# Attention of a Perceiver block: the score maxima of a batch in one VectorE operation over two PSUM banks

## The reference, cut to what matters

```
scores = einsum('bhsr,bhlr->bhsl', q_r, k_r)       # 16 heads x 32 tokens = 512 rows, 257 keys
attn   = softmax(scores, axis=-1)
ctx_c  = einsum('bhsl,bld->bhsd', attn, kv_rope)
out    = (ctx_c folded with w_kc_kv) @ Wo.T
x      = x + out
```

## Time and profile before

| | |
|---|---|
| median of 3 runs | 1026.26 us (1024.33 to 1026.9) |
| the profiled execution | 1022.87 us, of it a span of 1021.1 us between its first and last instruction |
| attention, from the first maxima to the last batch's exponentials | 139 to 362 us of the span |
| busy over the whole span | PE 94%, DVE 54%, ACT 41%, POOL 44% |

### The profile page before, as it was taken

The page is one execution under the profiler, slowest core; times in us unless marked ns, Lnnn a source line. Parts: engine busy times, 40 slices in busy tenths (PEclk is TensorE's granted clock), DMA queues, the critical chain, the costliest instruction groups (busy, mean ns, idle before and its releaser), DMA issues. The chain is left out here.

```text
span 1021.1 us, 15950 instructions
## 1 busy us (share of the span) xinstructions
PE 955.3 (94%) x5479; PEld 805.6 (79%) x5479; DVE 556.1 (54%) x1040; ACT 411.1 (40%) x954; POOL 453.3 (44%) x489
## 2 busy tenths in 40 slices
PE   4899976999999988999999999889999999999997
PEld 4677755888787866888888988677778899999997
DVE  6333468888899944444545332317968333333345
ACT  2333467677677734223432044352333122222111
POOL 1998845555576620000000302217614878993051
PEclk9999989999999999999999999999999999999999
DMA  6788702111111004422221014312023756661152
GB/s 221 231 269 264 225 13 93 35 40 42 32 37 38 27 27 130 139 83 82 82 89 36 3 59 138 102 29 81 2 85 113 262 171 235 202 225 63 42 159 99
DMA packets 79003, 109.91 MB, mean 108 GB/s; under 512 B 14224, under 2 KB 46992, under 8 KB 78928
## 3 DMA queue, kind: packets, MB, share of 16 engines
q1 hardware_dynamic: 66288, 82.18, 25.9%
q10 hardware_dynamic: 10080, 18.35, 5.0%
q0 software_dynamic: 2560, 8.39, 2.5%
HBM read 83.13 MB, written 25.77 MB: 107 GB/s over the span
## 5 line engine op out<-in xcount | busy, mean ns | idle before, releaser
L43 PE MATMUL psum<-second_xT_hi,second_w_hi 128*128 128x512 f32 x272 | 107.6, 396 | 7.0 <-DVE second_w_lo L1259 3.8
L45 PE MATMUL psum<-second_xT_hi,second_w_lo 128*128 128x512 f32 x272 | 106.6, 392 | 0.0
L44 PE MATMUL psum<-second_xT_lo,second_w_hi 128*128 128x512 f32 x272 | 106.5, 392 | 0.0
L1152 POOL TENSOR_TENSOR all_x<-all_x,mlp_raw 128x512 f32<-128x512 f32 x8 | 10.0, 1290 | 174.7 <-DVE all_x L1654 174.7
L2172 ACT ACTIVATE moe_s<-psum 128x352 f32<-128x352 f32 x39 | 18.1, 465 | 151.0 <-PE psum L45 151.0
L43 PEld LDWEIGHTS psum<-second_xT_hi,second_w_hi 128*128 128x128 f32 x272 | 51.4, 189 | 20.0 <-DVE second_w_lo L1259 5.3
L2238 DVE TENSOR_TENSOR moe_hT_lo<-psum,moe_hT_hi 128x384 fp32r<-128x384 f32 x39 | 21.8, 558 | 79.1 <-ACT moe_hT_hi L2178 79.1
L1609 ACT ACTIVATE mlp_s<-psum,mlp_side 128x512 f32<-128x512 f32 x32 | 21.8, 682 | 100.3 <-PE psum L45 100.3
L43 PE MATMUL psum<-moe_w_hi,moe_tT_hi 128*128 x184 | 61.3, 333 | 0.0
L1654 DVE TENSOR_TENSOR all_x<-all_x,psum 128x512 f32<-128x512 f32 x64 | 43.8, 687 | 31.7 <-PE psum L45 31.2
L45 PEld LDWEIGHTS psum<-second_xT_hi,second_w_lo 128*128 128x128 f32 x272 | 51.4, 189 | 11.0
(11 more groups left out here) (341 smaller groups left out, 2887.0 us busy)
## 6 DMA issues: line engine op xcount, KB each, us to landing
kv_all<-all_x ACTq DMA_DIRECT2D x28, 256.0 KB, 4.1
far_raw<-in_eg SPq DMA_DIRECT2D x10, 704.0 KB, 4.6
far_raw<-in_eu SPq DMA_DIRECT2D x10, 704.0 KB, 4.6
slot_rows<-mix_W SPq DMA_DIRECT2D x23, 256.0 KB, 5.9
slot_out<-far_rows ACTq DMA_DIRECT2D x23, 256.0 KB, 2.4
far_raw<-in_ed SPq DMA_DIRECT2D x10, 512.0 KB, 4.1
far_rows<-slot_rows ACTq DMA_DIRECT2D x19, 256.0 KB, 2.9
second_raw<-in_w_feat SPq DMA_DIRECT2D x18, 256.0 KB, 3.3
```

The source lines that it names most:

```text
L43: e.matmul(out, hi_l, hi_r, start=first, stop=False)
L44: e.matmul(out, hi_l, lo_r, start=False, stop=False)
L45: return e.matmul(out, lo_l, hi_r, start=False, stop=last)
L1152: pool.tensor_tensor(g["x"][:, t, :], g["x"][:, t, :], b2, ALU.add).then_inc(x_plus, 1)
```

## The change

The two reductions of 128x512 become one of 128x1024 over both banks, and the two clamps of two columns one clamp of four. The clamp's semaphore counts one for each batch, and ScalarE waits for it once, ahead of the first of the four exponentials. Both pairs' scores must be there before the reduction starts. TensorE's matmuls, banks and waits stay as they are.

```
-        def scores_of(b, i):
-            return psum[:, SC + 2 * (b % 2) + i, :].rearrange("p (j k) -> p j k", k=LM)
+        def scores_of(b):
+            bank = SC + 2 * (b % 2)
+            return psum[:, bank:bank + 2, :].rearrange("p i (j k) -> p (i j) k", k=LM)
...
                 wait(act, pt_ready, b - 1)
+                act.wait_ge(low_ok, b + 1)
                 for j in range(NJ):
-                    act.wait_ge(low_ok, 2 * b + j // 2 + 1)
-                    act.activation(pr(b)[:, j, :], scores_of(b, j // 2)[:, j % 2, :], ACT.Exp, bias=low[:, p, j:j + 1],
+                    act.activation(pr(b)[:, j, :], scores_of(b)[:, j, :], ACT.Exp, bias=low[:, p, j:j + 1],
...
-            def maxima(b, i):
-                v.wait_ge(sc_ready, 2 * b + i + 1)
-
-                wait(v, exp_ok, NJ * (b - 2) + 2 * i + 2)
-                v.tensor_reduce(pair(low, b, i), scores_of(b, i), AX_X, ALU.max, negate=True).then_inc(top_ok, 1)
-                v.wait_ge(top_ok, 2 * b + i + 1)
-                v.tensor_scalar(pair(low, b, i), pair(low, b, i), 0.0, None, ALU.min).then_inc(low_ok, 1)
+            def maxima(b):
+                v.wait_ge(sc_ready, 2 * (b + 1))
+
+                wait(v, exp_ok, NJ * (b - 1))
+                v.tensor_reduce(low[:, b % 2, :], scores_of(b), AX_X, ALU.max, negate=True).then_inc(top_ok, 1)
+                v.wait_ge(top_ok, b + 1)
+                v.tensor_scalar(low[:, b % 2, :], low[:, b % 2, :], 0.0, None, ALU.min).then_inc(low_ok, 1)
...
-                    maxima(s, 0)
-                    maxima(s, 1)
+                    maxima(s)
```

More of the change, by code:

```diff
@@ L827, in scores @@
                         rows = slice(j * P, (j + 1) * P)
-                        m = passes(pe, scores_of(b, i)[:, j % 2, :], q_hi[:, p, rows], q_lo[:, p, rows],
+                        m = passes(pe, scores_of(b)[:, j, :], q_hi[:, p, rows], q_lo[:, p, rows],
                                    kvT[:, p, 0, :], kvT[:, p, 1, :], True, True)
```

## The result

The changed kernel takes 1046.89 us in the median (1042.89 to 1051.3, 6 runs) against 1025.45 (1024.16 to 1026.9, 6 runs): slower by 2.1%, ratio 1.0212 with a 95% interval of 1.0195 to 1.0229. That is +21.4 us; the prediction's sum was +22.4.

The account below looks back on a forecast made before the run. Bound: a ring over VectorE and ScalarE, TensorE hardly faster. Terms 15.1 + 0.4 + 1.0 + 3.9 + 2.0 = 22.4, called 22, added to the median 1026.3 gave 1048 us; 1033 to 1056 held 8 in 10.

Parts of the forecast that it names:

- The ring: Attention: work passing between VectorE and ScalarE sets the pace, 6.56 us a slot, through the first exponential; 7.64 after the change.
- The tie: Clamp starts at +2.65 after the second reciprocal, GpSimd's queries_lo at +2.63; the clamp is held until +3.95.
- normal slot: Slots 2 to 6, 8, 9, 11 to 13, 15 to 17, 29: each grows by 1.08 us, together 15.1.
- The two ties of the earlier trace: Before the change, clamps starting 0.00 and 0.01 behind GpSimd's L787 and L247 lasted as long: 0.74 and 1.28 us.
- The rival of a clamp that slips in: The clamp gets in ahead of GpSimd's queries_lo and ends at +2.82; sum +2.7 us, time 1029; chance 0.13.
- slots 21, 23, 25, 27, 28: Slots with a norm piece on GpSimd holding up VectorE: 7.64 us replaces 6.87, 3.9 in all.
- slots 0 and 1: First two attention slots: first exponential later, partly given back; estimated at 2.0 us together, between 0 and 4.
- the seven counted at nothing: Slots 7, 19, 20, 22, 24, 26 and 31: something else already late or no queries to split; up to 1.08 each possible.
- What hides behind it: Nothing behind the attention can absorb the loss of 22 us; everything there is only shifted.
- TensorE's wait for L973: TensorE's waits in the attention for VectorE's L973 (the old L972) grow from 11.5 us by some 20.
- The rival that VectorE's work is the bound: Attention: the change takes 1.13 of 2.55 us out of a slot's maxima; -8 us, time 1018; chance 0.04.
- The lock: A two-port tensor_scalar on VectorE and a GpSimd operation exclude each other for a whole instruction; tensor_reduce never takes part.

Follow-up runs that it names:

- e2: The kernel before (two reductions, two clamps), with both clamps as tensor_reduce in place of tensor_scalar: 1015.46 us, ratio 0.9902.
- k248: The changed kernel with the maximum taken over 248 of the 256 keys, so a slightly shorter reduction: 1047.26 us, ratio 1.0209.
- k240: The changed kernel with the maximum taken over 240 of the 256 keys, so a shorter reduction: 1037.45 us, ratio 1.0103.
- e1: The changed kernel with its one clamp as a tensor_reduce in place of the tensor_scalar: 1028.23 us, ratio to before 1.0036.
- e3: The changed kernel with GpSimd's long operation queries_lo moved ahead of its short columns_lo: 1031.76 us, ratio 1.0077.
- e6: The changed kernel with the clamp of four columns cut into four tensor_scalar operations of one column each: 1031.46 us, ratio 1.0065.

## Why the prediction was right

**The ring.** Right. The time came from the ring over VectorE and ScalarE, which was read off one slot; TensorE, within 0.1 us of it (6.47 in slots 21 to 28 of e2), had to wait as soon as it grew.

**The reduction.** 1.21 was taken, 1.217 measured.

**The tie.** Right, and the point on which all hung: clamp at +2.65, L793's record 0.03 ahead of it, and held. 19 of 32 clamps last 1.22 to 1.30, where "some 20" were forecast. The phase isn't the same in every normal slot, as the prediction had it: in slots 2 and 5 the reduction waits for scores and the clamp starts 0.61 and 0.27 into L793. It ends with L793 all the same, and these slots take 7.60 and 7.62 too. The two ties of the earlier trace rows were the right guide, but the margin was small. A clamp 0.01 ahead of L793's record is still held (k248, and slot 19 of k240), one 0.02 ahead is free (slot 3 of k240), and the prediction's own range for the reduction, down to 1.16, would have put the clamp 0.03 ahead.

The rival of a clamp that slips in had been priced by a reduction of 1.16; k240's takes 1.15 and it does slip in. The price was too low: 1029 was forecast for such a kernel, 1037 came out. TensorE's pace throws the clamps of slots 5, 9, 12 and 16 back into L793, and the slots 21, 23, 25 and 27 take 7.6, where the rival left them at 6.87. The rival's arithmetic also took the free clamp's end at +2.82 from the reduction of 1.21; with 1.16 it is +2.77 and the slot 6.46, near k240's 6.43.

**The sum, term by term**, against the reciprocals of the trace:

| | forecast | trace |
|---|---|---|
| 14 normal slots | 15.1 | 15.1 (6.53 to 6.64 became 7.60 to 7.88) |
| slots 10 and 14 | 0.4 | 0.4 |
| slots 18 and 30 | 1.0 | 1.0 |
| slots 21, 23, 25, 27, 28 | 3.9 | 3.8 |
| slots 0 and 1 | 2.0 | 1.3 |
| the seven counted at nothing | 0 | -0.3 (slots 22 and 26, -0.2 each) |
| sum | 22.4 | 21.4 |

The terms of the trace add up to 21.35 before rounding. The one term well off is that of slots 0 and 1, an estimate and called one. Why slots 22 and 26 got shorter was not followed up. The sum of the trace (without the 2.7 us from ahead of the attention) agrees with the measured difference of the medians, 21.4.

**What hides behind it.** Right: nothing behind the attention took any of it back (24.06 us from the start to the last second reciprocal, 24.0 over the span). TensorE's clock did not fall further, 0.97 in the window before and after. TensorE's wait for L973 did not grow by 20 as forecast. By name it went from 11.5 to 13.4. But waits of the same matmuls for which the view names no releaser ("issue") went from 2.5 to 17.7:

```profile
PE psum L43 <- issue: 17.7, 24, 1.1
PE psum L43 <- DVE first_xT_lo L973: 13.4, 5, 3.5
```

```profile
206.52 0.47 PE L43 MATMUL psum<-first_xT_lo,first_xT_hi 128*128 128x512 f32 x1 [0.91 <-issue]
```

The last row, from the timeline, is one of these waits, in slot 9. The matmul reads what L973 wrote, and starts 0.10 after the second L973 ends at 206.42. So at least this wait is one for L973, and both kinds together grew by 17.1.

**The rival that VectorE's work is the bound.** Wrong, as held: VectorE's busy time fell from 196.3 to 188.0 in a window that got 21.4 us longer. The Trainium skill's rule that a larger tile pays the fixed cost once (VectorE: DVE Perf Modes, the errata section) is told there of operations that read SBUF, where these reductions read PSUM. Here too one large reduction was cheaper than two, 1.217 against twice 0.679, by 0.14 us of VectorE's time a slot that nobody waits for.

**The lock.** The Trainium skill's statement (SBUF — State Buffer, "Who interferes with whom") agrees with the runs on the two operations compared: `tensor_scalar` on four columns is held by L793, `tensor_reduce` in the same place is not (e1). It doesn't fit the records of GpSimd's L210, which hold no clamp (last section).

## What to carry to other kernels

Where two engines hand work to each other in a ring, ask of a merging when the first result comes that the other engine waits for. Here the merging saved work and the result came later: 0.53 us a batch without the port (e1 against e2), 1.25 with it (first exponential at +4.04, not +2.79). Before an instruction is moved on VectorE, look at what GpSimd is doing at the place where it will land: a 0.17 us clamp may cost 1.3 us, and it is worth writing it in a form that doesn't share the port, as e2 does for 1% of the whole time. When a forecast hangs on a tie of hundredths, look for earlier ties of the same two engines in the trace of before.

## What was not expected of the hardware

A clamp that starts 0.02 to 0.05 ahead of L793's record is free, one that starts 0.01 ahead or in the same hundredth is held for all of it (k240, k248). A clamp that has long been waiting for one GpSimd operation isn't held by the next one, though the records of the two have no gap (e3). In the changed kernel, though, the clamp starts while L788's record has 0.01 or 0.02 to go, and L793 still holds it. One pattern covers all of these (L210, below, aside): the next GpSimd operation holds the clamp unless the clamp started at least 0.02 before that operation's record, whether it is running or waiting by then. No run tests what lies behind it.

A record of GpSimd is not always a held port. In the changed kernel the clamp of slot 30 starts 0.56 us into L210, a `pow` on two columns, and is free (GpSimd, then VectorE); the same holds for the clamps of slots 18, 22 and 26:

```profile
374.06 0.70 POOL L210 TENSOR_TENSOR att_rstd<-att_var,edge_power 128x2 f32<-128x2 f32 x1
```

```profile
374.62 0.17 DVE L956 TENSOR_SCALAR att_low<-att_low 128x4 f32<-128x4 f32 x1
```

Why this one differs from L793 was only seen, not tested: its size and its operation both do. And a `tensor_scalar` on one column is not held in any of 128 cases in e6, at places where one on four columns is.
